# Sixteen heads instead of twice eight: scale-and-mask and maxima in the last layer's attention

## The reference, cut to what matters

```python
def attention(q, k, v, mask):                       # q, k, v: (b, 16 heads, 128, 16)
    scores = jnp.einsum('bhqd,bhkd->bhqk', q, k) / jnp.sqrt(jnp.float32(HD))
    scores = scores * mask - 10000.0 * (1.0 - mask)
    probs = jax.nn.softmax(scores, axis=-1)
    return jnp.einsum('bhqk,bhkd->bhqd', probs, v)

ctx = merge_heads(attention(split_heads(q), split_heads(k), split_heads(v), ltor_mask))
x = hidden_states + ctx @ w_ao + b_ao               # then layernorm, and the same once more
```

## Time and profile before

| what | value |
|---|---|
| median of 3 runs | 1434.52 us (1434.38 to 1435.5) |
| the profiled execution | 1433.1 us |
| its span, first to last instruction | 1431.3 us |
| mean granted TensorE clock | 0.958 |
| PE busy | 1299.8 us (91%) |
| DVE busy | 826.7 us (58%) |
| ACT busy | 741.6 us (52%) |
| POOL busy | 542.9 us (38%) |
| stage a5, first scale to last sum | from 1187.71 to 1258.71 us |
| stage a6 | from 1292.93 to 1364.02 us |

### The profile page before, as it was taken

The page is one execution under the profiler, slowest core; times in us unless marked ns, Lnnn a source line. Parts: engine busy times, 40 slices in busy tenths (PEclk is TensorE's granted clock), DMA queues, the critical chain, the costliest instruction groups (busy, mean ns, idle before and its releaser), DMA issues.

```text
span 1431.3 us, 24249 instructions
## 1 busy us (share of the span) xinstructions
PE 1299.8 (91%) x8912; PEld 1016.8 (71%) x8912; DVE 826.7 (58%) x1900; ACT 741.6 (52%) x2037; POOL 542.9 (38%) x605
## 2 busy tenths in 40 slices
PE   6999999999879968999999779999997986786789
PEld 5777777777545546999999669999984655645637
DVE  4666666766559964666666636666664027728710
ACT  4655555555427855555555445555544245746640
POOL 3554545444349955222111222211102037538520
PEclk9999999999998997999999989999998998978989
DMA  6101010100010011111111001121001010000000
GB/s 245 47 25 49 25 49 25 49 25 27 3 60 0 2 61 45 38 38 46 63 42 38 8 30 45 38 68 38 9 1 59 0 59 1 1 16 1 1 0 30
DMA packets 15379, 50.41 MB, mean 35 GB/s; under 512 B 1824, under 2 KB 5152, under 8 KB 14240
## 3 DMA queue, kind: packets, MB, share of 16 engines
q1 hardware_dynamic: 15264, 48.87, 10.2%
HBM read 47.82 MB, written 1.05 MB: 34 GB/s over the span
## 4 chain that ended last, share of the span: by engine, by line
PE 80%; DVE 12%; ACT 3%; issue 2%; POOL 2%; DMA 0%; SPq 0%; DVEq 0%; POOLq 0%
PE pS L1610 13%; PE pT L1638 6%; PE acc L313 6%; PE acc L1689 6%; PE pC L376 5%; PE pT L363 4%; PE acc L1418 4%; PE pS L346 4%; PE pC L1674 4%; PE acc L332 4%; PE pS L1653 4%; DVE stats L1282 3%; PE acc L919 3%; PE acc L388 3%; PE heads_transposed L1125 2%
## 5 line engine op out<-in xcount | busy, mean ns | idle before, releaser
L1610 PE MATMUL pS<-split_sources,split_pair_weights 128*128 128x512 f32 x768 | 214.9, 416 | 15.2 <-POOL split_sources L1991 7.7
L663 POOL TENSOR_TENSOR probs<-probs,stats 128x512 f32<-128x512 f32 x128 | 130.4, 1040 | 182.1 <-DVE stats L541 182.1
L484 ACT ACTIVATE probs<-pS,stats 128x256 f32<-128x256 f32 x256 | 118.1, 473 | 135.8 <-DVE stats L536 135.8
L1610 PEld LDWEIGHTS pS<-split_sources,split_pair_weights 128*128 128x128 f32 x768 | 138.4, 193 | 42.4 <-POOL split_sources L1991 8.2
L1760 ACT ACTIVATE probsT<-pT 128x256 f32<-128x256 f32 x128 | 49.3, 385 | 199.7 <-PE pT L1664 199.7
L1927 POOL TENSOR_TENSOR split_pair_weights<-weights_a,split_pair_weights 128x1024 fp32r<-128x1024 f32 x16 | 35.1, 2192 | 280.1 <-ACT split_pair_weights L1769 280.0
L1689 PE MATMUL acc<-l_wo_parts,l_ctx_parts 128*128 128x256 f32 x768 | 122.9, 296 | 0.4 <-DVE l_ctx_parts L1865 0.4
L1638 PEld LDWEIGHTS pT<-l_wv_parts,split_sources 128*128 128x128 f32 x756 | 108.8, 192 | 17.1 <-ACT probsT L1760 5.7
L536 DVE TENSOR_REDUCE stats<-pS 128x2 f32<-128x512 f32 x128 | 82.4, 686 | 61.6 <-PE pS L346 61.5
L1638 PE MATMUL pT<-l_wv_parts,split_sources 128*128 128x256 f32 x756 | 113.1, 285 | 3.8 <-ACT probsT L1760 3.8
L313 PE MATMUL acc<-split_sources,split_pair_weights 128*128 128x512 f32 x372 | 102.1, 410 | 1.0 <-POOL split_pair_weights L650 0.7
(11 more groups left out here) (215 smaller groups left out, 2928.1 us busy)
## 6 DMA issues: line engine op xcount, KB each, us to landing
weights_a<-in_l_w SPq DMA_DIRECT2D x16, 771.0 KB, 4.3
weights_a<-in_l_w SPq DMA_DIRECT2D x16, 768.5 KB, 4.4
weights_b<-in_l_wo SPq DMA_DIRECT2D x16, 257.0 KB, 2.7
value_bias_rows<-in_l_bv SPq DMA_DIRECT2D x16, 256.0 KB, 4.5
w_fc<-in_l_w SPq DMA_DIRECT2D x4, 1024.0 KB, 6.0
bias_rows<-in_rows SPq DMA_DIRECT2D x1, 1536.0 KB, 13.3
x_residual<-in_x_dbl SPq DMA_DIRECT2D x2, 512.0 KB, 6.9
masked_scores<-in_ctx_dbl SPq DMA_DIRECT2D x2, 512.0 KB, 7.8
```

Of the source, the lines that this page charges most:

```text
L484: a = e.activation(self.E[:, n % 4, h, it, :], self.S[h][:, it, :], ACT.Exp, bias=self.st[:, 1, n % 4, h, it:it + 1], accum_out=self.st[:, ...
L663: e.tensor_tensor(self.E[:, n % 4, h, :, :], self.E[:, n % 4, h, :, :], self.st[:, 3, n % 4, h, :].unsqueeze(2).broadcast_to([P, 2, D]), A ...
L1610: mm = e.matmul(bank[:, :], self.w_qk[i % 2][kw][:, 1 - which, c, h * P:h * P + P], g.split[:, which, ks, c, half * HALF:half * HALF + HAL ...
```

## The change

In stages a5 and a6 `scale_and_mask` and `maxes` each become one instruction over all sixteen heads where they were two over eight. `self.parts` goes, and with it the semaphore counts by halves: POOL's masks of a round wait for the scaling of the whole round, the maxima for all four of the masks, both halves of the exps and POOL's shift for the maxima of the whole round. In DVE's step the whole scaling of round t now stands ahead of the maxima of round t-1. Layer 1 already ran in one part and is as it was.

```diff
@@ def __init__
-        self.parts = 2 if multiply else 1
-        H = self.parts
...
@@ def pool
         def add_masks(r, c):
             b = 0 if self.one_mask else self.unit(r)[0]
-            wait(e, self.scaled, 2 * r + c // 2 + 1)
+            wait(e, self.scaled, r + 1)
...
         def shift(r, c):
-            wait(e, self.nmax, self.parts * (r + 1))
+            wait(e, self.nmax, r + 1)
@@ def pe, scores(r)
             if r >= 1:
-                wait(e, self.scaled, self.parts * r)
+                wait(e, self.scaled, r)
@@ def act, exps(r, half)
-                wait(e, self.nmax, 2 * r + half + 1)
+                wait(e, self.nmax, r + 1)
@@ def dve
-        def scale_and_mask(r, part=0):
+        def scale_and_mask(r):
             b = 0 if self.one_mask else self.unit(r)[0]
-            n = 4 // self.parts
-            if part == 0:
-                wait(e, self.s_full, r + 1)
-                if r >= 3:
-                    wait(e, self.t_full, 2 * (r - 3) + 2)
-            e.scalar_tensor_tensor(out=self.heads(self.sm[r % 3])[:, 4 * n * part:4 * n * (part + 1), :],
-                                   in0=self.heads(self.bS[:, n * part:n * (part + 1), :]
-                                                  .rearrange("p c t -> p (c t)")),
+            wait(e, self.s_full, r + 1)
+            if r >= 3:
+                wait(e, self.t_full, 2 * (r - 3) + 2)
+            e.scalar_tensor_tensor(out=self.heads(self.sm[r % 3]),
+                                   in0=self.heads(self.bS[:, :, :].rearrange("p c t -> p (c t)")),
                                    scalar=self.scale,
-                                   in1=g.mask[:, b, :].unsqueeze(1).broadcast_to([P, 4 * n, P]),
+                                   in1=g.mask[:, b, :].unsqueeze(1).broadcast_to([P, 16, P]),
...
-        def maxes(r, part=0):
-            n = 16 // self.parts
+        def maxes(r):
             if self.multiply:
-                wait(e, self.masked, 4 * r + 2 * part + 2)
+                wait(e, self.masked, 4 * r + 4)
...
-            e.tensor_reduce(self.nm[r % 3][:, n * part:n * (part + 1)],
-                            self.heads(self.sm[r % 3])[:, n * part:n * (part + 1), :], AX.X, ALU.max,
-                            negate=True).then_inc(self.nmax.sem, 1)
+            e.tensor_reduce(self.nm[r % 3], self.heads(self.sm[r % 3]), AX.X, ALU.max, negate=True)\
+                .then_inc(self.nmax.sem, 1)
...
+                if t < self.R:
+                    scale_and_mask(t)
                 if 0 <= t - 1 < self.R:
-                    maxes(t - 1, 0)
-                if t < self.R:
-                    scale_and_mask(t, 0)
-                if 0 <= t - 1 < self.R:
-                    maxes(t - 1, 1)
-                if t < self.R:
-                    scale_and_mask(t, 1)
+                    maxes(t - 1)
```

More of the change, by code:

```diff
@@ L1005, in __init__ @@
          self.xb, self.ct_full, self.cx, self.o_full, self.x) = g.counts(
-            "small_heads", keys_masked=0 if multiply else R, scores_in_bank=R, scores_scaled=H * R,
-            scores_masked=4 * R if multiply else 0, negmax_ready=H * R,
+            "small_heads", keys_masked=0 if multiply else R, scores_in_bank=R, scores_scaled=R,
+            scores_masked=4 * R if multiply else 0, negmax_ready=R,
             scores_shifted=R if multiply else 4 * R, exp_ready=2 * R, transposed_in_bank=2 * R,
```

## The result

The changed kernel takes 1448.78 us (median of 4 runs, 1446.77 to 1449.84), the kernel before 1434.45: a ratio of 1.0098, 95% interval 1.008 to 1.0115, 14.3 us slower. The forecast was 1444.5 with a range up to 1448.0. The profiled execution took 1448.97 us, its span is 1447.2 us, 15.9 more than that of before, at a mean granted clock of 0.948 instead of 0.958.

The account below looks back on a forecast made before the run. It took POOL's masks to bound a stage's start, DVE its middle, and PE, ACT and DVE in turn its end. Profiled 1433.1 + 6.6 hand-offs + 3.4 clock = 1443.1, plus 1.4 to the median: 1444.5 us, range 1439.0 to 1448.0.

Parts of the forecast that it names:

- DVE's width (1): DVE's scale and maxima in stages a5, a6: two wide instructions save 0.12 us per round, at most 1.9 us over 16.
- The start (2, 3): Stage start: masks(0) about 1.0 us later, exp(0) waits for all maxima, scale(3) 0.5 us later before any clock effect.
- The rounds (4): Middle rounds: the loop from sum through scores, scale and maxima takes 6.74 us, more than 6.60; later rounds gain nothing.
- The last round (5): Stage end: masks(7) wait for whole scale(7), exp(7) for whole max(7); with earlier terms 3.3 us per stage, 6.6 for both.
- The clock (6): PE at stage start: clock rises late, transposes(0) and scores(3) run slow; 1.7 us per stage, 3.4 for both.
- rival D: PE's clock also falls sooner at the thin end of a stage: 1448.5 us; chance 0.07.
- B: DVE's busy time alone decides, late maxima covered elsewhere: 1432.6 us, no measurable change; chance 0.10.
- C: PE's late scores, not POOL's masks, held the stage start, so a stage wins 1.8 us: 1430.9 us; chance 0.05.
- A: Hand-offs cost as forecast but PE's clock rises as before: 1441.1 us; chance 0.20.

Follow-up runs that it names:

- long fill: Changed kernel plus extra identity transposes on PE in its long gaps, 40 instead of 16 of them ahead of transposes(0): 1438.95 us, ratio 1.0042 to before.
- round 7 in halves: Changed kernel with the maxima of round 7 alone again two instructions over eight heads: 1448.29 us, ratio 1.0108 to before.
- rounds 6 and 7: Changed kernel with the maxima of rounds 6 and 7 again two instructions over eight heads each: 1442.33 us, ratio 1.0057 to before.
- with fill: Changed kernel plus extra identity transposes on PE ahead of scores(1), (2) and transposes(0), (1), (2), (6), 16 of them ahead of transposes(0): 1443.25 us.
- whole maxima: Kernel before in the new order, scaling still in two halves, maxima one instruction over sixteen heads: 1443.67 us, ratio 1.0072 to before.
- maxima in halves: Changed kernel with the maxima again two instructions over eight heads with own semaphore counts, scaling still whole: 1436.68 us, ratio 1.0025 to before.

## Why the prediction was wrong

It was right in the direction and in how the loss begins, and too low: 10.0 us forecast over the run, 14.3 measured, 0.8 us outside the range.

**DVE's width (1).** Right: 2.28 to 2.29 us for the wide instructions, DVE's busy time down by 0.8 us a stage. It brought nothing to the end of the stage.

**The start (2, 3).** Right. Masks(0) came 1.07 us later relative to the first scale (1.0 forecast), exp(0) at 9.75 us behind it, transposes(0) 3.3 us behind scores(2). With the late rise of the clock scale(3) was to come 2.2 us later; it came 2.23 later. The split of that sum is less sure: with the long fill scale(3) came 0.03 us later than before, where the hand-offs alone were to cost 0.5.

**The rounds (4).** The loop over sum, scores, scale and maxima was given as 6.74 us; it is 6.73.

**The last round (5).** Right where the clock is held, and hidden in the changed kernel. With the long fill exp(7) starts 3.26 us later than before behind the first scale (forecast 3.4), transposes(7) 3.11 (3.3), and exp(7) waits for max(7). In the changed kernel another chain ends later, and this one the prediction did not have: exp(6) starts only behind scale(7) and max(6) both whole, 4.52 us behind scale(7)'s start (1234.27 to 1238.79), where it was 1.99 (1230.62 to 1232.61), 2.5 us later. From before:

```profile
1232.61 3.61 ACT L1204 ACTIVATE masked_scores<-masked_scores,stats 128x128 f32<-128x128 f32 x12
```

Behind exp(6) come transposes(6) and the context of round 5 at the low clock, then ACT's copy of that context and exp(7). So the run with round 7 in halves moved nothing, and that with rounds 6 and 7 did. The two chains are close: with the long fill the one over max(7) ends only 0.37 us later than the other, and halves in rounds 6 and 7 gain 1.0 us a stage there.

**The clock (6).** This is the step that failed, by its size. I had the clock rise late once, 1.7 us per stage, with a bound of twice that. That late rise came as described. But the same waits opened more gaps in PE's work, and the clock fell twice more in each stage: ahead of transposes(2) PE was idle for 2.29 us, ahead of transposes(6) for 1.44 (after 0.42 just before). These steps ran at 1.97 and 1.93 us instead of 1.06, the contexts right behind them at 1.57 and 1.64 instead of 1.08. The runs with fill give the sizes. At the sixth sum the changed kernel is 6.85 and 6.98 us behind before, with the fill that prevents these two falls 5.05 and 4.79, with the long fill 3.14 and 2.99. That makes 1.8 and 2.2 us for the two falls and 1.9 and 1.8 for the start: the clock cost 3.7 and 4.0 us in the stages, where the term had 1.7 each. Another 1.6 us came behind stage a6, where the clock rose later. A window of before, just ahead of the last MLP's long run of matmuls, and one of after:

```profile
1372.00:1376.00 4.00, 3.96 (x10) 1.94 (x10) 0.00 (x0) 3.57 (x7) 4.00 (x7) 0.74 0.02 4
```

```profile
1388.00:1392.00 4.00, 4.00 (x7) 1.68 (x6) 0.00 (x0) 1.99 (x3) 2.98 (x5) 0.55 0.00 0
```

Before, the clock was up again about 10.5 us behind the last sum of a6, after about 13.7. That this makes the 1.6 us is read from the windows; no run changed it alone. The rival D had more of the low clock, at 1448.5 us, but put it at the thin end of the stage, with a chance of 0.07. It had the sum and not the place: at the thin end the clock did no worse than before.

**The rivals.** B (no change) and C (faster) fell: with the clock held, both stages are still longer and the kernel slower by 5.1 us. A (no late clock) is near what the long fill made: 5.1 us above before, where A had 6.6. That low clock costs time in the changed kernel is shown by the fills and by the two unequal stages of the run with whole maxima; how the 9 us of the profiled 15.9 that are not hand-offs split over its places is taken from differences between these runs, one profile each.

## What to carry to other kernels

Look at what waits for a wide instruction's last element before counting what its width spares: here 0.12 us a round was to be won on DVE, and exp(6) lost 2.5 us against scale(7). When a wait moves by a microsecond or two, go through every gap that it opens on PE in every round, not just the first, and price each at both clocks. Compare stages at a point ahead of the places where the clock differs from run to run: whole lengths mixed two effects here, in most of the runs. Where PE runs thin before a dense stretch, a few useless matmuls can be worth more than a spared instruction.

## What the runs showed of the hardware

The same work at two levels of the granted clock differed by 3.75 us in one execution (77.36 and 73.61 us, maxima whole). The length of a gap alone does not tell whether the clock falls: 1.43 us of idle ahead of transposes(6) stood in both of these stages, with a fall in one. Sixteen extra transposes ahead of an idle stretch of 3.33 us did not keep the clock at 1.00; forty, 4.59 us of work that ended 0.7 us ahead of the next, did. PE's low clock reaches far beyond the change: with the same instructions the stretch between the last sum of a5 and the first scale of a6 took 34.6 us in the changed kernel and the one before, 32.3 with maxima in halves and 32.5 with fill.
